# Cross-attention and gated feed-forward on one core: first tile in banks of its own, gate and up steps over four PSUM banks, and activations 32 bytes further on

## The chip, the cores and the metric

The kernel runs on one core of a Trainium2 chip. The metric is the device time of one execution in microseconds, the median of several runs. Before the change it is 1023.58 us, the median of 3 runs (1022.61 to 1025.23).

## The reference

The input is x (32 batches of 128 rows, 256 wide), a context (32 x 128 x 512) and a row mask. Everything is float32.

```python
# cross-attention, 8 heads of 32
t   = layernorm(x)
src = (ctx @ W_src.T + b_src) * mask        # 512 wide: k | v
q   = (t   @ W_tgt.T + b_tgt) * mask
p   = softmax(where(mask_of_key == 0, -inf, q @ k.T / sqrt(32)))
x1  = x + concat(t, p @ v) @ W_out.T + b_out
# feed-forward, hidden width 1024, weights of -1, 0, 1 with a scale s per output
n   = layernorm(x1)
h   = silu(n @ w1.T * s1) * (n @ w2.T * s2)
h   = gelu(h @ h1.T * t1)
h   = gelu(h @ h2.T * t2)
out = x1 + h @ w3.T * s3
```

## The kernel before, in words

**Tiles.** Two batches of 128 rows make a tile of 256 rows (T), so there are 16 tiles. Two streams of work are interleaved: the feed-forward of tile f, the attention of tile a = f + 1, and the projections of tile n = f + 2. Each engine has its own list of instructions, written out by hand; semaphores tie them together. PER (before line 30) says how far a tile moves each semaphore, and at(name, tile, k) is the value to wait for.

**TensorE.** For a tile f, gates_part issues the scores of tile a, then four gate_up steps. A step q computes two blocks of 128 gate columns into bank F[0] and two up blocks into F[1], 8 matmuls each: two blocks, two slices of 128 of the contraction, and a high and a low part. The activations are kept as two float32r tensors (x2h and x2l; hAh and hAl; hBh and hBl) whose sum is the float32 value, while the ternary weights W1, W2, H1, H2, W3 are exact in float32r. Then come transposes_x(n), project_k(n), project_q(n) and project_v(n) in float32. They use the banks G[0] (transposes, q) and G[1] (k, v). middle_part(f) has eight steps of 32 float32r matmuls (q from 4 to 11, banks F[q % 2]), with attend(a) and out_proj(a) ahead of q = 8 and transpose_x2(a) ahead of q = 10, then ffn_out(f). The eighth bank group S takes four banks for the scores.

**Waits of the gate steps.** gate_up(q) waits for sil_ready up to 2q before it writes F[0] again, and for g_ready up to 2q before it writes F[1] again. project_k waits for x1_ready of two tiles before, transposes_x for x2_ready.

**ScalarE.** silu(f, q) (lines 605 to 609), copies of PSUM (copy_xnT, keep_xnT, scale_v, copy_upd, x2_hi), the exponentials exps(a, j) (line 635) and gelu(f, q) (line 616). Each change of function set loads a table (ACT_TABLE_LOAD). silu waits for gate_done first and for g_ready second.

**VectorE.** In the gates' stretch of tile f: keep_residual (line 723), mask_scores(a, 0) (778), gate_times_up (840) for the pairs of blocks, split (857 and 859, the copy that rounds to float32r and the subtraction that gives the low part), then row_max(a, 0) (782, 786), bias_mask_k(n) (754) and the rest of the softmax: normalise (790, 793) and turn_blocks (805), whose result goes through DRAM and back (turn_p on SyncE) to be transposed.

**GpSimd.** The powers -1/2 of both LayerNorms (987, 998), add_bias (994), and in the first tiles the copies cast (1012), which turn each raw float32 weight chunk into float32r in place.

**The start.** The weights come in 22 chunks of 512 KB (4 of W1 and W2, which are EARLY, 8 of H1, 8 of H2, 2 of W3). Before a chunk is cast, an engine looks at the low 16 bits of its elements: look on ScalarE (667) for 19 of them, on VectorE (874) for chunks 9 to 11. count_low_bits, sum_low_bits (1002) and raise_flag (884) make of it two flags, one for the early chunks and one for all. TensorE loads each flag (585, 593) and branches to a float32r or a float32 version of the program. Tile 0 and tile 1 have their own order: first_gates holds the transposes of the probabilities of tile 0 (394), its attention and output projection in G[0] and G[1], projections of tile 1, and then gates_part(0, 1, 2). Tile 1's x and context are loaded into the home of hBh. All transfers are issued on SyncE's queue; its loads start at line 264, s3 is issued last (291).

Of the kernel before, what the change touches and what calls it, by code (L numbers as in the profile page):

```python
# [12 lines left out]
NB = 2  # L13
# [9 lines left out]
WARM = 10  # L23
MASKED = -3.0e38
# [7 lines left out]
    pb_ready=2, p_written=16, p_loaded=64, av_done=1, upd_ready=1,  # L32
    o_done=1, x1_ready=1, stats2=4, veps2=1, rstd2=1, xn2_ready=2, x2t_done=1, x2hi_ready=1, x2_ready=1,
# [5 lines left out]
def program(nc, x, ctxT, mask_row, mask_col, wsT, wvT, wtT, woT, b_cols, b_v, b_out, w1T, w2T, h1T, h2T,  # L39
            w3T, s_cols, s3, out):  # L40
    st = ExitStack()
    with st:
# [49 lines left out]
        hBl = sb("hBl", [P, KH, T], F32R)  # L92
        g, sil = sb("g", [P, 2, 2, T]), sb("sil", [P, 2, T])
# [3 lines left out]
        x_in_1 = tile1_home[:, KC:KC + NB * D // T, :]  # L97

# [3 lines left out]
        def x_of(a):  # L102
            return x_in_1 if isinstance(a, int) and a == 1 else x_in[:]

        F = [st.enter_context(nc.psum_tensor(f"F{i}", [P, 2, T], F32)) for i in range(2)]
# [3 lines left out]
        p_banks = [[F[c][:].rearrange("p h t -> p (h t)") for c in range(KD)],  # L109
                   [S[:, c].rearrange("p j c s -> p (j c s)") for c in range(KD)]]  # L110
# [4 lines left out]
        x_loaded = sem("x_loaded")  # L115
        ctx_loaded = sem("ctx_loaded")
        mrow_loaded = sem("mrow_loaded")
        mcol_loaded = sem("mcol_loaded")
# [83 lines left out]
        on_dve = [9, 10, 11]  # L202
        on_act = [n for n in range(CHUNKS) if n not in on_dve]
# [9 lines left out]
        def _(sp):  # L213
# [4 lines left out]
            def load_mask_row(m):  # L218
                sp.wait_ge(kT_ready, at("kT_ready", m - 1, 2))
                sp.wait_ge(qT_ready, at("qT_ready", m - 1, 2))  # L220
                sp.wait_ge(mask_bias_ready, at("mask_bias_ready", m - 1, 1))
                sp.dma_start(mrow[:], mask_row[bass.ds(m, 1)].broadcast_to([P, T])).then_inc(mrow_loaded, 16)
# [5 lines left out]
            def load_x(m):  # L228
                sp.wait_ge(xn_ready, at("xn_ready", m - 1, 2))
                sp.wait_ge(xb_ready, at("xb_ready", m - 1, 2))  # L230
                sp.dma_start(x_in[:], x[bass.ds(m, 1)].rearrange("o p n -> (o p) n")).then_inc(x_loaded, 16)
# [34 lines left out]
            sp.dma_start(WK[:], wsT).then_inc(wk_loaded, 16)  # L266
            sp.dma_start(bcols[:], b_cols).then_inc(bias_loaded, 16)
            sp.dma_start(mrow[:], mask_row[0:1].broadcast_to([P, T])).then_inc(mrow_loaded, 16)
# [3 lines left out]
            sp.dma_start(mcol[:], mask_col[0]).then_inc(mcol_loaded, 16)  # L272
            sp.dma_start(bv_bc[:], b_v.broadcast_to([P, D])).then_inc(bv_loaded, 16)
            sp.wait_ge(x_loaded, 16)
            sp.dma_start(x_in_1, x[1]).then_inc(x_loaded, 16)
            sp.wait_ge(ctx_loaded, 16)
            sp.dma_start(cT_1.rearrange("p k t -> p (k t)"), ctxT[1]).then_inc(ctx_loaded, 16)
            load_chunks(range(EARLY))
            sp.dma_start(WO[:], woT).then_inc(wo_loaded, 16)
            load_chunks(range(EARLY, EARLY + KH))  # L280
            load_mask_row(1)
            sp.wait_ge(x_loaded, 32)
            sp.wait_ge(xn_ready, at("xn_ready", 0, 2))
            sp.wait_ge(xb_ready, at("xb_ready", 0, 2))
            sp.dma_start(x_in[:], x[2]).then_inc(x_loaded, 16)
            sp.wait_ge(ctx_loaded, 32)
            sp.wait_ge(v_done, at("v_done", 0, 1))
            sp.dma_start(cT[:], ctxT[2]).then_inc(ctx_loaded, 16)
# [795 lines left out]
```

## Time and profile before

| | |
|---|---|
| median of 3 runs | 1023.58 us |
| the profiled execution, its own time | 1028.29 us |
| its span, first to last instruction | 1026.5 us |
| TensorE busy | 962.8 us, 7716 matmuls |
| VectorE, ScalarE, GpSimd busy | 597.4, 393.8, 68.8 us |
| granted TensorE clock, mean | 0.982 |
| moved by DMA | 64.56 MB |

The profile comes from one execution; its time is 4.7 us above the median of the runs shown. A share of the span is an average over the start (about 130 us with gaps) and fifteen tiles that look alike. Where a line of the timeline ends in brackets, they hold the idle time of the engine just before it and what ended it. Matmuls overlap in the pipeline, so the step from one's start to the next's counts, not the duration of one.

### The profile page before, as it was taken

To read this page: it belongs to the slowest core of one execution; us is meant where nothing else is said; L and a number is where in the kernel's file an instruction comes from. 1 tells how busy PE (TensorE), PEld (TensorE's weight loads), DVE (VectorE), ACT (ScalarE), POOL (GpSimd) and SP (SyncE) were. 2 spreads that over 40 slices of the span, in tenths; PEclk is the share of its full clock that TensorE was granted. 3 is DMA by queue.
4 is the path that set the end of the run, shared out by engine and by line. 5 is a ranking of instruction groups with operands and counts; after the bars stand their busy time and mean duration, and the time that the engine had idled before them with its cause. 6 is when DMAs were issued, how large, how long until landed. Compare 5 with 4: busy or idle time off the path is not lost.

```text
span 1026.5 us, 20570 instructions
## 1 busy us (share of the span) xinstructions
PE 962.8 (94%) x7716; PEld 909.0 (89%) x7716; DVE 597.4 (58%) x1143; ACT 393.8 (38%) x1081; POOL 68.8 (7%) x95
## 2 busy tenths in 40 slices
PE   7667899999999999999999999999999999997998
PEld 6567889999898999989899998989999898997888
DVE  4557375575847557484655748466574746657342
ACT  4446243352524335252342525334252533425221
POOL 2133000001000000100001010000101000000000
PEclk9788999999999999999999999999999999999999
DMA  9702103030120303012030301203020130202000
GB/s 335 308 5 83 38 11 109 21 107 10 56 72 10 107 20 107 10 56 72 10 107 20 102 15 46 82 10 107 20 92 26 34 94 10 82 11 76 8 11 11
DMA packets 51438, 64.56 MB, mean 63 GB/s; under 512 B 6736, under 2 KB 43984, under 8 KB 51408
## 3 DMA queue, kind: packets, MB, share of 16 engines
q1 hardware_dynamic: 51408, 64.15, 19.0%
q8 instruction: 20, 0.33, 0.1%
q14 instruction: 10, 0.08, 0.0%
HBM read 44.21 MB, written 19.92 MB: 62 GB/s over the span
## 4 chain that ended last, share of the span: by engine, by line
PE 84%; issue 5%; ACT 4%; DMA 3%; DVE 2%; SPq 1%; ACTq 0%; POOL 0%; DVEq 0%
PE F L456 56%; PE G L438 6%; PE F L525 6%; PE G L370 5%; PE G L348 4%; PE G L359 2%; ACT sil L609 2%; PE S L383 2%; PE G L419 1%; DMA p_dram<-pb 1%; DMA W_raw<-w 1%; ACT pr L635 1%; DVE pr L793 1%; PE G L335 1%; PE G L448 1%
## 5 line engine op out<-in xcount | busy, mean ns | idle before, releaser
L456 PE MATMUL F<-hAh,H 128*128 128x256 f32 x1024 | 251.5, 287 | 11.6 <-POOL H L1012 6.0
L456 PE MATMUL F<-hBh,H 128*128 128x256 f32 x1024 | 250.9, 287 | 0.7 <-DVE hBl L859 0.7
L456 PE MATMUL F<-hAl,H 128*128 128x256 f32 x1024 | 248.1, 284 | 0.0
L616 ACT ACTIVATE g<-F,scols 128x256 f32<-128x256 f32 x256 | 107.2, 471 | 365.8 <-PE F L456 365.6
L456 PE MATMUL F<-hBl,H 128*128 128x256 f32 x1024 | 246.9, 283 | 0.0
L456 PEld LDWEIGHTS F<-hAh,H 128*128 128x128 f32 x1024 | 197.7, 193 | 13.7 <-POOL H L1012 6.4
L456 PEld LDWEIGHTS F<-hAl,H 128*128 128x128 f32 x1024 | 197.8, 193 | 0.3
L456 PEld LDWEIGHTS F<-hBh,H 128*128 128x128 f32 x1024 | 196.1, 192 | 1.3 <-DVE hBl L859 0.9
L456 PEld LDWEIGHTS F<-hBl,H 128*128 128x128 f32 x1024 | 196.3, 192 | 0.4
L456 PE MATMUL F<-x2h,W 128*128 128x256 f32 x512 | 132.8, 298 | 20.5 <-ACT sil L609 18.8
L456 PEld LDWEIGHTS F<-x2h,W 128*128 128x128 f32 x512 | 96.8, 189 | 32.6 <-ACT sil L609 26.1
L456 PE MATMUL F<-x2l,W 128*128 128x256 f32 x512 | 125.5, 282 | 0.0
L635 ACT ACTIVATE pr<-pr,nmx 128x128 f32<-128x128 f32 x256 | 99.1, 388 | 36.8 <-DVE nmx L786 36.8
L857 DVE CAST hAh<-g 128x512 fp32r<-128x512 f32 x128 | 54.0, 422 | 100.6 <-ACT g L616 100.6
L456 PEld LDWEIGHTS F<-x2l,W 128*128 128x128 f32 x512 | 97.1, 190 | 0.0
L857 DVE CAST hBh<-g 128x512 fp32r<-128x512 f32 x64 | 27.2, 426 | 114.1 <-ACT g L616 114.1
L859 DVE TENSOR_TENSOR hAl<-g,hAh 128x512 fp32r<-128x512 f32 x128 | 88.7, 693 | 4.4
L840 DVE SCALAR_TENSOR_TENSOR g<-F,scols,sil 128x256 f32<-128x256 f32 x128 | 56.1, 479 | 58.9 <-PE F L456 39.0
L609 ACT ACTIVATE sil<-F,scols 128x256 f32<-128x256 f32 x128 | 53.7, 470 | 73.4 <-PE F L456 73.2
L525 PE MATMUL F<-W,hAh 128*128 128x256 f32 x256 | 62.1, 283 | 0.0
L525 PE MATMUL F<-W,hAl 128*128 128x256 f32 x256 | 62.1, 283 | 0.0
L998 POOL TENSOR_TENSOR rs<-ve,neg_half 128x2 f32<-128x2 f32 x16 | 11.0, 690 | 692.1 <-DVE ve L820 692.1
(93 smaller groups left out, 1250.2 us busy)
## 6 DMA issues: line engine op xcount, KB each, us to landing
p_dram<-pb SPq DMA_DIRECT2D x30, 512.0 KB, 3.2
pr<-p_dram SPq DMA_DIRECT2D x120, 128.0 KB, 2.6
H_raw<-h SPq DMA_DIRECT2D x16, 512.0 KB, 15.6
cT<-ctx_t SPq DMA_DIRECT2D x15, 512.0 KB, 3.5
out<-y SPq DMA_DIRECT2D x32, 128.0 KB, 1.7
x_in<-x_t SPq DMA_DIRECT2D x15, 256.0 KB, 2.6
W_raw<-w SPq DMA_DIRECT2D x6, 512.0 KB, 10.3
mrow<-mask_row SPq DMA_DIRECT2D x16, 128.0 KB, 3.2
```

The source lines that it names most:

```text
L348: ins = mm(G[1][:, c * T:(c + 1) * T], WK[:, k, c * P:(c + 1) * P], cT_of(a)[:, k, :], start=k == 0, stop=k == KC - 1)
L359: ins = mm(G[0][:, c * T:(c + 1) * T], WQ[:, k, c * P:(c + 1) * P], xnT[:, k, :], start=k == 0, stop=k == KD - 1)
L370: ins = mm(G[1][:, j * D:(j + 1) * D], cT_of(a)[:, k, j * P:(j + 1) * P], WV[:, k, :], start=k == 0, stop=k == KC - 1)
L438: ins = mm(G[1][:, j * D:(j + 1) * D], lhsT, WO[:, k, :], start=k == 0, stop=k == 2 * KD - 1)
L456: return mm(bank, W[0][:, k, cols], part[:, k, :], start=first, stop=last)
L525: ins = mm(F[j][:, 0, :], lhsT, W3[:, k, :], start=first, stop=last)
L609: fn(sil[:, p % 2, :], F[0][:, p % 2, :], ACT.Silu, scale=scols[:, p:p + 1]).then_inc(sil_ready, 1)
L616: fn(g[:, q % 2, m, :], F[q % 2][:, m, :], ACT.Gelu, scale=scols[:, col:col + 1]).then_inc(gelu_ready, 1)
L635: ins = fn(pr[j][:, r, c, :], pr[j][:, r, c, :], ACT.Exp, bias=nmx[:, j, h:h + 1], scale=SCALE, accum_out=den[:, j, h:h + 1])
L840: V.scalar_tensor_tensor(g[:, q % 2, p % 2, :], F[1][:, p % 2, :], scols[:, KH + p:KH + p + 1], sil[:, p % 2, :], ALU.mult, ALU.mult).then ...
L857: V.tensor_copy(hi[:, pair, :], g[:, q % 2, :, :]).then_inc(hi_ready, 1)
L859: V.tensor_tensor(lo[:, pair, :], g[:, q % 2, :, :], hi[:, pair, :].bitcast(F32), ALU.subtract).then_inc(h_ready, 1)
```

## The change

1. **Four banks for gate and up.** Steps q = 0 and 2 write gate and up into G[0] and G[1], steps 1 and 3 into F[0] and F[1]. A step from q = 2 on waits for the SiLU and product of two steps before. sil has four places instead of two. transposes_x(n) and project_k(n) now wait for all sil_ready and g_ready of the tile. silu and gelu have their waits in the other order. VectorE's order is product, split, product, split, product, row_max(a, 0), product, split, split, mask_scores(a, 1).
2. **First tile.** Its attention, output projection and second LayerNorm go batch by batch (j = 0, 1), in banks of their own: tail_banks are two banks of S, o_banks are G[0] and G[1]. Semaphores from av_done to x2_ready count two per tile. Projections q and v and the scores of tile 1 move behind the gates of tile 0, project_k is cut into two halves.
3. **Looks.** ScalarE looks at 14 chunks, VectorE at eight (3, 7, 11, 17 to 21), placed between other work. The casts are in the order of the chunks. The order of the first loads changes; tile 1's mask row gets its own place.
4. **A pad** of 8 float32 (32 bytes) stands before x2h, so x2h, x2l, hA, hB, g, sil and y start 32 bytes further on.

```diff
+PAD = 8
+        sb("pad", [P, PAD])
         x2h, x2l = sb("x2h", [P, KD, T], F32R), sb("x2l", [P, KD, T], F32R)
...
-        g, sil = sb("g", [P, 2, 2, T]), sb("sil", [P, 2, T])
+        hBl, mrow_home = with_raw("hBl", KH, T)
+        g, sil = sb("g", [P, 2, 2, T]), sb("sil", [P, 4, T])
...
+        tail_banks = [s_bank(2), s_bank(3)]
+        o_banks = [G[0], G[1]]
+        def gate_banks(q):
+            if q % 2:
+                return F[0][:], F[1][:]
+            return G[0][:].rearrange("p (h t) -> p h t", h=2), G[1][:].rearrange("p (h t) -> p h t", h=2)
...
-        on_dve = [9, 10, 11]
-        on_act = [n for n in range(CHUNKS) if n not in on_dve]
+        on_act = [0, 1, 2, 4, 5, 6, 8, 9, 10, 12, 13, 14, 15, 16]
+        on_dve = [3, 7, 11, 17, 18, 19, 20, 21]
...
@@ sync: first loads
             sp.dma_start(WV[:], wvT).then_inc(wv_loaded, 16)
+            load_chunks(range(EARLY))
+            sp.dma_start(bv_bc[:], b_v.broadcast_to([P, D])).then_inc(bv_loaded, 16)
+            sp.dma_start(mcol[:], mask_col[0]).then_inc(mcol_loaded, 16)
+            sp.dma_start(x_in_1, x[1]).then_inc(x_loaded_1, 16)
+            sp.dma_start(cT_1.rearrange("p k t -> p (k t)"), ctxT[1]).then_inc(ctx_loaded_1, 16)
             sp.dma_start(bo_bc[:], b_out.broadcast_to([P, D])).then_inc(bo_loaded, 16)
             sp.dma_start(WO[:], woT).then_inc(wo_loaded, 16)
+            sp.dma_start(mrow_1, mask_row[1:2].broadcast_to([P, T])).then_inc(mrow_loaded_1, 16)
+            load_chunks(range(EARLY, EARLY + 4))
+            sp.dma_start(scols[:], s_cols).then_inc(scales_loaded, 16)
+            load_chunks(range(EARLY + 4, EARLY + KH))
             sp.wait_ge(v_done, at("v_done", 0, 1))
+            load_x(2)
             sp.dma_start(cT[:], ctxT[2]).then_inc(ctx_loaded, 16)
+            load_mask_row(2)
             load_chunks(range(EARLY + KH, CHUNKS))
...
@@ tensor: project_k, transposes_x
-                    pe.wait_ge(x2_ready, at("x2_ready", a - 2, 1))
+                    pe.wait_ge(sil_ready, at("sil_ready", a - 2, KH))
...
-                    pe.wait_ge(x1_ready, at("x1_ready", a - 2, 1))
+                    pe.wait_ge(g_ready, at("g_ready", a - 2, KH))
...
@@ tensor: gate_up
-                    pe.wait_ge(sil_ready, at("sil_ready", f, 2 * q))
+                elif q > 1:
+                    pe.wait_ge(sil_ready, at("sil_ready", f, 2 * q - 2))
...
-                    pe.wait_ge(g_ready, at("g_ready", f, 2 * q))
+                elif q > 1:
+                    pe.wait_ge(g_ready, at("g_ready", f, 2 * q - 2))
...
@@ tensor: gates_part of tile 0, first_gates
+                if first:
+                    project_q(1)
+                    scores(1)
+                    project_v(1)
...
                 transpose_p_0(0)
+                out_proj_x_0(0)
+                out_proj_x_0(1)
+                transpose_p_0(1)
+                attend_0(0)
+                attend_0(1)
+                out_proj_u_0(0)
+                out_proj_u_0(1)
                 transposes_x(1)
+                project_k(1, 0)
+                transpose_x2_0(0)
+                transpose_x2_0(1)
+                project_k(1, 1)
                 gates_part(0, 1, 2, general)
...
@@ scalar: silu
+                    act.wait_ge(g_ready, at("g_ready", f, max(p - 3, 0)))
+                    act.wait_ge(gate_done, at("gate_done", f, q + 1))
+                    fn(sil[:, p % 4, :], gate_bank[:, p % 2, :], ACT.Silu, scale=scols[:, p:p + 1]).then_inc(sil_ready, 1)
...
@@ vector: tile
+                if first:
+                    ln1_stats(2)
                 gate_times_up(f, 0)
+                split(f, 0)
                 gate_times_up(f, 1)
+                split(f, 1)
                 gate_times_up(f, 2)
+                if a is not None and not first:
+                    row_max(a, 0)
+                if first:
+                    ln1_apply(2)
+                    look(17)
                 gate_times_up(f, 3)
                 split(f, 2)
+                if first:
+                    look(18)
                 split(f, 3)
+                if first:
+                    look(19)
+                    bias_mask_q(1)
+                    mask_scores(1, 0)
+                    row_max(1, 0)
                 if a is not None:
+                    mask_scores(a, 1)
...
@@ gpsimd: start
             inverse_std1(0)
+            for n in range(EARLY):
+                cast(n)
+            sum_low_bits(0)
             add_bias(0)
             inverse_std1(1)
+            inverse_std2_0(0)
+            inverse_std2_0(1)
+            for n in range(EARLY, EARLY + 4):
+                cast(n)
+            inverse_std1(2)
+            for n in range(EARLY + 4, EARLY + KH):
+                cast(n)
             add_bias(1)
+            for n in range(EARLY + KH, CHUNKS - 2):
+                cast(n)
             sum_low_bits(1)
```

## Rows read from the trace of the kernel before

**Rows 1.** The page: busy time of each engine; GB/s in 40 slices of 25.7 us.

```profile
PE 962.8 (94%) x7716; PEld 909.0 (89%) x7716; DVE 597.4 (58%) x1143; ACT 393.8 (38%) x1081; POOL 68.8 (7%) x95
...
GB/s 335 308 5 83 38 11 109 21 107 10 56 72 10 107 20 107 10 56 72 10 107 20 102 15 46 82 10 107 20 92 26 34 94 10 82 11 76 8 11 11
```

**Rows 2.** Timeline of TensorE, one repeating tile: start us, us, engine, line, operation.

```profile
256.25 0.38 PE L456 MATMUL F<-x2h,W 128*128 128x256 f32 x1
...
257.42 0.28 PE L456 MATMUL F<-x2l,W 128*128 128x256 f32 x1
...
258.14 0.28 PE L456 MATMUL F<-x2l,W 128*128 128x256 f32 x1
...
259.75 0.39 PE L456 MATMUL F<-x2h,W 128*128 128x256 f32 x1 [1.34 <-ACT sil L609]
...
266.30 0.60 PE L335 MATMUL G<-ident,xn 128*128 128x128 f32 x4
266.74 3.62 PE L348 MATMUL G<-cT,WK 128*128 128x256 f32 x16
270.19 1.89 PE L359 MATMUL G<-xnT,WQ 128*128 128x256 f32 x8
...
316.49 0.38 PE L456 MATMUL F<-x2h,W 128*128 128x256 f32 x1
```

**Rows 3.** Timeline of TensorE, the start.

```profile
35.06 1.94 PE L394 MATMUL F<-ident,pr 128*128 128x128 f32 x8 [9.08 <-issue]
...
53.93 0.39 PE L456 MATMUL F<-x2h,W 128*128 128x256 f32 x1 [0.31 <-DVE x2l L832]
...
87.72 0.55 PE L456 MATMUL F<-hAh,H 128*128 128x256 f32 x1 [6.00 <-POOL H L1012]
...
108.93 0.93 PE L419 MATMUL G<-pr,v 128*32 128x128 f32 x16 [3.13 <-DMA pr<-p_dram]
```

**Rows 4.** Timeline of ScalarE in the tile of rows 2.

```profile
257.56 1.28 ACT L609 ACT_TABLE_LOAD   x1 [5.23 <-PE F L456]
...
267.63 1.28 ACT L635 ACT_TABLE_LOAD   x1
271.06 0.40 ACT L635 ACTIVATE pr<-pr,nmx 128x128 f32<-128x128 f32 x1 [2.15 <-DVE nmx L786]
```

**Rows 5.** Timeline of VectorE in the tile of rows 2.

```profile
256.72 1.22 DVE L778 TENSOR_TENSOR pr<-S,mbias 128x1024 f32<-128x1024 f32 x1
...
264.31 0.88 DVE L840 SCALAR_TENSOR_TENSOR g<-F,scols,sil 128x256 f32<-128x256 f32 x2 [0.33 <-PE F L456]
265.11 0.42 DVE L857 CAST hAh<-g 128x512 fp32r<-128x512 f32 x1
...
268.44 0.42 DVE L857 CAST hAh<-g 128x512 fp32r<-128x512 f32 x1
...
269.51 1.21 DVE L782 TENSOR_REDUCE mx<-pr 128x8 f32<-128x1024 f32 x1
...
271.12 0.88 DVE L754 SCALAR_TENSOR_TENSOR kT<-G,bcols,mrow 128x256 f32<-128x256 f32 x2
```

**Rows 6.** SyncE's issue of the last first load, s3, and its time to landing.

```profile
35.18 1.11 SPq L291 DMA_DIRECT2D s_bc<-s  x1
...
DMA to landing us min/median/max: 14.9/14.9/14.9
```

**Rows 7.** Timeline of VectorE, the start: looks, second flag, one normalise.

```profile
40.20 3.46 DVE L874 TENSOR_REDUCE low_bits<-H_raw 128x1 f32<-128x1024 uint16 x3
...
82.96 0.14 DVE L884 TENSOR_SCALAR flag<-most 1x1 int32<-1x1 f32 x1 [0.42 <-POOL most L1002]
...
86.89 6.96 DVE L793 TENSOR_TENSOR pr<-pr,rden 128x1024 f32<-128x1024 f32 x1
```

**Rows 8.** Timeline of GpSimd, the last casts.

```profile
82.89 7.91 POOL L1012 CAST H<-H_raw 128x1024 fp32r<-128x1024 f32 x8
90.75 2.02 POOL L1012 CAST W<-W_raw 128x1024 fp32r<-128x1024 f32 x2
```

More of the change, by code:

```diff
@@ L378, in scores @@
                 pe.wait_ge(masked, at("masked", a - 1, 2))
+                if isinstance(a, int) and a == 1:
+                    pe.wait_ge(x2_ready, at("x2_ready", 0, 2))
                 for j in range(NB):
@@ L529, in gates_part @@
             def gates_part(f, a, n, general):
-                if a is not None:
+                first = isinstance(f, int) and f == 0
+                if a is not None and not first:
                     scores(a)
@@ L582, in _ @@
             project_v(0)
-            project_k(1)
             pe.wait_ge(flag_ready, 1)
@@ L668, in look, with tile @@
                        accum_out=low_bits[:, n:n + 1]).then_inc(act_looked, 1)
-            def tile(f, a, n, looks=()):
+            def tile(f, a, n):
+                first = isinstance(f, int) and f == 0
                 for q in range(4):
                     silu(f, q)
-                if n is not None:
+                    if first:
+                        look(on_act[6 + 2 * q:8 + 2 * q])
+                if not first and n is not None:
                     copy_xnT(n)
-                look(looks)
                 if a is not None:
@@ L884, in raise_flag, with tile @@
                 V.tensor_scalar_min(flag[:, i:i + 1], most[:, i:i + 1], 1.0).then_inc(flag_ready, 1)
-            def tile(f, a, n, m, late_flag=False):
+            def tile(f, a, n, m):
+                first = isinstance(f, int) and f == 0
                 keep_residual(f)
-                if a is not None:
+                if a is not None and not first:
                     mask_scores(a, 0)
+                if first:
+                    ln1_stats(2)
                 gate_times_up(f, 0)
+                split(f, 0)
                 gate_times_up(f, 1)
-                split(f, 0)
+                split(f, 1)
                 gate_times_up(f, 2)
-                split(f, 1)
+                if a is not None and not first:
+                    row_max(a, 0)
+                if first:
+                    ln1_apply(2)
+                    look(17)
                 gate_times_up(f, 3)
                 split(f, 2)
+                if first:
+                    look(18)
                 split(f, 3)
-                if late_flag:
-                    ln1_stats(n)
-                    ln1_apply(n)
-                if a is not None:
-                    row_max(a, 0)
+                if first:
+                    look(19)
+                    bias_mask_q(1)
+                    mask_scores(1, 0)
+                    row_max(1, 0)
+                if a is not None:
+                    mask_scores(a, 1)
+                if first:
+                    row_max(1, 1)
+                    bias_v(1)
+                    for c in on_dve[6:]:
+                        look(c)
                 if n is not None:
                     bias_mask_k(n)
-                if a is not None:
-                    mask_scores(a, 1)
+                if a is not None and not first:
                     row_max(a, 1)
```

382 lines of the change are left out of this document (216 added, 166 removed).

## The prediction

> **What bounds the kernel now.** I read the page first, then the timeline of one repeating tile engine by engine, then the start up to 136 us. TensorE is busy 94% of the span [rows 1], so a term counts only if it takes idle time from TensorE or makes its instructions shorter. Both are to be seen in the tile that starts at 256.25 [rows 2]: from 257.42 to 258.14 six float32r matmuls go by, 0.12 us each; the second gate step waits 1.34 us for the SiLU that still reads its bank; the first matmul of project_k runs at 266.74, 10.49 us after the first gate matmul. The next tile starts at 316.49, so a tile takes 60.24 us. The idle time of the start comes in larger pieces: gaps of 9.1, 6.0 and 3.1 us [rows 3].
>
> **Part 1, four banks for gate and up (tiles 1 to 13).** The 64 matmuls of the gates need 64 x 0.12 = 7.7 us; before they take 10.05 (266.30 - 256.25), so 2.3 us of waits are in reach. In the new order of waits the gate's own wait stands last, on the activation itself. That is how exps is written, and there the table load runs at 267.63, straight behind the copy, while the activation waits until 271.06 [rows 4]. So I let the 1.28 us load of Silu (257.56, after the gate was done) vanish behind idle ScalarE time, and the first SiLU start 1.4 us after the tile instead of 2.6.
> But TensorE then meets a new wait. project_k writes G[1], which is now an up bank, and needs all eight g_ready, given by VectorE. VectorE in the tile's first stretch, in start-to-start steps of [rows 5], from tile start: the residual's copy; mask_scores 0.47 to 1.71 (1.22 and a step); first gate_times_up when the first up step is done, 16 matmuls and 0.28 of drain, 2.25, and 0.80 long: 3.05; split 1.07 (268.44 to 269.51): 4.12; second up product 4.15 to 4.95; split 6.02; third 6.08 to 6.88; the row_max that is put in here, 269.51 to 271.12 = 1.61 (less 0.1): 8.4; fourth 9.2. project_k starts at 9.25 and its first matmul 0.1 later, 9.35 against 10.49: **1.14 us per tile, not 2.3**; the other half comes back as this wait of about 1.3 us, between the transposes (done at 8.4) and project_k. Queued behind it are project_q and project_v, which just shift with it. VectorE runs on without a gap to kT: splits to 11.3, mask_scores to 12.6, while project_k ends at 9.35 + 16 x 0.216 + 0.4 = 13.2. 13 x 1.14 = 14.8 us.
> Tile 14 has no next projection and tile 15 no attention: the middle steps start at the last split. Before, that is 13.3 after tile start (269.51 - 256.25); after, 9.2 + 2.1 = 11.3 for tile 14 and 11.0 for tile 15, whose VectorE is free of mask and maximum. 2.0 + 2.3 = 4.3 us. Sum of this part -19.1 us.
>
> **Part 2, the start.** TensorE stands 9.1 us before 35.06 [rows 3], for the first flag and the branch on it. The change puts this flag earlier: the four early chunks are issued ahead of x[1], cT[1] and two bias loads, 1.0 MB, 3.0 us at the 335 GB/s of the page's first slice [rows 1]; normalise (1.2) goes behind the flag, as does add_bias(0) on POOL, and a look of 1.15 comes before it. I put the flag 3 us earlier. Own banks then shorten transposes, attention, output projection and LayerNorm, and the gates could start near 47 instead of 53.93. This gain is mostly not collected: VectorE waits for s3 before tile 0, s3 is the last transfer, it lands at 35.18 + 14.9 = 50.1 [rows 6], and nothing is taken out of that queue; SyncE's new order (mask row 1 into a place of its own without a wait, x[2] and cT[2] after the first v_done, scols up front) only turns loads around within it. So VectorE starts tile 0 at 50.1; before it started with the gates, at 53.8.
> From there VectorE and TensorE go in turns, with the durations of [rows 2, 5] (a look 3.46 / 3 = 1.15 [rows 7]): four products, four splits, ln1 of tile 2 and looks 17 to 19 end at 63.4; qT(1) 64.3; scores 65.5; masks and maxima 71.1; V(1), at twice 0.216 for half of it since TensorE stood before, 71.1, vb 71.9; K(2) 75.5; exps and the three copies on ScalarE 76.8; Q(2) 78.7; normalise and flag 81.5; V(2) 82.2. The branch on the second flag, written at 83.1 [rows 7], costs what it does now, 87.72 - 83.1 = 4.6: middle steps at 86.7, before 87.72, **-1.0 us**. The wait of attend for its DMA, 3.1 us [rows 3], goes, since that normalise was held until 93.9 and will run at about 84: **-3.1 us**.
> Against it stands a hold on VectorE. normalise at 86.89 takes 6.96 us [rows 7] instead of 1.22, while POOL casts without a pause from 82.89 to 92.77 [rows 8]. In the changed kernel POOL's casts 8 to 14 and add_bias(1) are let go by inverse_std1(2), and this follows ln1_stats(2) on VectorE, right before split(0,0), which subtracts two SBUF tiles. POOL has seven casts of 1.04 and 1.5 us of bias ready then, 8.8 us. Bounds: 0, if POOL leaves pauses, and 8.8. I take what the one row of such a hold shows, 6.96 - 1.22 = 5.7: **+5.7 us**. The head comes to +1.6. The Trainium skill (page "SBUF — State Buffer", section "Who interferes with whom") says that a VectorE instruction with two SBUF inputs and a GpSimd one that reads SBUF can't run together, and that the one which comes second waits for the whole of the other. By that rule, one cast at a time, the hold would be about 1 us and the sum 1001; the 6.96 us, longer than any single cast, don't agree with it.
> Looks themselves: ScalarE gives up five of them, which hides behind the banks' waits; VectorE takes five more, and they are in the list above.
>
> **Part 3, 32 bytes.** Adding up the tensors in order, each rounded up to 32 bytes, x2h, x2l, hA, hB, g, sil and y start on multiples of 64 before and 32 beyond one after; W1 to W3 stay on multiples of 64. So moving and stationary operand stop being alike in position in all 352 float32r matmuls of a tile, 5632 in all. No row has a float32r matmul so placed. The nearest, in float32: project_k, moving cT at 32 and WK at 0, 0.216 us each (3.62 - 0.38 for 15 steps); project_q, both at 0, also 0.216, from 1.89 - 0.38 for 7 [rows 2]. They say nothing happens, and I take **0**. But float32r stands at 0.12 where a float32 transpose of 128 columns, its moving identity at 32 and its stationary xn at 0, steps 0.11 (0.44 for four, 266.30 to 266.74). So the gain is bounded by 0.12 - 0.108 = 12 ns, half of 0.216. A loss isn't excluded; I give it the same 12 ns.
>
> **The sum.** -19.1 + 1.6 = -17.5 us on the profiled execution, 1028.29 (span 1026.5 and 1.8 around it): 1010.8. That execution stands 4.7 above the median 1023.58 of the runs; carried over, 1006.
>
> **Rivals.**
> A, no hold: POOL leaves a gap and VectorE isn't stopped. Against it: normalise's 6.96 us [rows 7]. 1006 - 5.7 = 1000.
> B, the 32 bytes do it: something between the two operand streams costs 12 ns per matmul now. For it: the 0.12 against 0.108. The gates' 64 gain nothing (VectorE sets project_k's start), 288 x 16 x 12 ns = 55 us: 951; a third of it 988. The Trainium skill (page "TensorE: Matmul & The Clock Gate", section "Back-to-back issue gap") gives 262 cycles for 256 moving columns, 109 ns; this case's 120 differs from it, and the measurement decides. By that figure there would be 11 ns to win somewhere.
> C, the steady gain is lost: the load of the Silu table stays behind the gate's wait (0.9 us later for the first product and so for project_k) or VectorE needs 1.1 us more. For it: every step there is tight. 1006 + 14.8 = 1021.
> D, the other side: the shifted operands slow the float32r stream. It decides from 17.5 / 5632 = 3.1 ns on; at 12 ns 1006 + 55 = 1061. Against it: the float32 rows, and no row that is slower by position.
> That the change doesn't do what it says: the pad might move tensors that no bank or port cares about. That is the forecast's own case for part 3.
>
> **The numbers.** Forecast 0.40, A 0.15, B 0.28, C 0.12, D 0.05. About 0.3% (3 us) is what a measurement tells from no change: forecast, A, B and most of C lie beyond, so faster 0.91; same 0.05, from C and the small end of D; slower 0.04. The range goes down to B's full price, 948, and up to 1018, the forecast with 8.8 us of hold and half of C; the forecast's own range is 998 to 1014.
>
> **What would show it.** Project_k's first matmul at 9.3 after tile start with g_ready as its releaser, and the Silu load before the gate is done: part 1. If K comes at 8.5, VectorE isn't the limit. VectorE's first subtraction of tile 0 lasting some us under casts: the hold. First look: the step between float32r matmuls. If it isn't 0.12, the forecast is wrong by 4.6 us for each ns.

## The result, and the profile after

The changed kernel takes 997.86 us, the median of 4 runs (995.59 to 998.0), against 1024.18 for the kernel before beside it on the same chip (4 runs, 1022.61 to 1025.23): a ratio of 0.9734 with a 95% interval of 0.9713 to 0.9755. It is faster, 8 us beyond the forecast of 1006 and inside its range. The profiled execution has a span of 996.0 us against 1026.5.

The page after, the line that answers to the first of [rows 1]: TensorE has lost 29.6 us of busy time with the same 7716 matmuls, nearly the whole 30.5 us by which the span is shorter. So most of the gain isn't idle time that the page shows; either the instructions became shorter or they waited less while they counted as busy.

```profile
PE 933.2 (94%) x7716; PEld 887.0 (89%) x7716; DVE 601.4 (60%) x1151; ACT 388.5 (39%) x1073; POOL 72.3 (7%) x96
```

Timeline of TensorE after, one repeating tile (start us, us, engine, line, operation; answers to [rows 2]):

```profile
250.90 0.38 PE L519 MATMUL G<-x2h,W 128*128 128x256 f32 x1
251.12 0.28 PE L519 MATMUL G<-x2l,W 128*128 128x256 f32 x1
...
251.82 0.28 PE L519 MATMUL G<-x2l,W 128*128 128x256 f32 x1
...
258.69 0.66 PE L372 MATMUL G<-ident,xn 128*128 128x128 f32 x4
260.64 3.69 PE L386 MATMUL G<-cT,WK 128*128 128x256 f32 x16 [1.29 <-DVE g L964]
...
309.36 0.38 PE L519 MATMUL G<-x2h,W 128*128 128x256 f32 x1
```

The tile takes 309.36 - 250.90 = 58.46 us instead of 60.24. The gates need 7.8 us instead of 10.05 (from 250.90 to the transposes at 258.69). The 1.34 us wait for the SiLU is gone, and a wait of 1.29 us for VectorE's last product stands ahead of project_k, which starts 9.74 us after the start of its tile instead of 10.49. From 251.12 to 251.82 six steps take 0.70 us, where [rows 2] show 0.72 for six; experiment 1 reads this over sixty.

The SiLUs and their table load in the same tile after (answers to [rows 4]); and VectorE's part (answers to [rows 5]):

```profile
246.98 1.28 ACT L689 ACT_TABLE_LOAD   x1
252.14 0.84 ACT L689 ACTIVATE sil<-G,scols 128x256 f32<-128x256 f32 x2 [3.88 <-PE G L519]
```

```profile
251.37 1.22 DVE L875 TENSOR_TENSOR pr<-S,mbias 128x1024 f32<-128x1024 f32 x1
253.27 0.88 DVE L964 SCALAR_TENSOR_TENSOR g<-G,scols,sil 128x256 f32<-128x256 f32 x2 [0.69 <-PE G L519]
254.18 0.43 DVE L983 CAST hAh<-g 128x512 fp32r<-128x512 f32 x1
254.65 0.69 DVE L985 TENSOR_TENSOR hAl<-g,hAh 128x512 fp32r<-128x512 f32 x1
255.25 0.87 DVE L964 SCALAR_TENSOR_TENSOR g<-F,scols,sil 128x256 f32<-128x256 f32 x2
...
257.23 0.87 DVE L964 SCALAR_TENSOR_TENSOR g<-G,scols,sil 128x256 f32<-128x256 f32 x2
258.02 1.21 DVE L879 TENSOR_REDUCE mx<-pr 128x8 f32<-128x1024 f32 x1
...
259.61 0.88 DVE L964 SCALAR_TENSOR_TENSOR g<-F,scols,sil 128x256 f32<-128x256 f32 x2
```

The table load runs 4 us before the tile begins, as forecast. VectorE goes in the order forecast, without a gap from 253.27 on.

TensorE in the start after (answers to [rows 3]); no idle time stands before attend at 109.03 any more:

```profile
30.75 1.94 PE L434 MATMUL F<-ident,pr 128*128 128x128 f32 x8 [11.66 <-issue]
...
45.94 0.47 PE L519 MATMUL G<-x2h,W 128*128 128x256 f32 x1
...
69.06 2.09 PE L424 MATMUL S<-kT,qT 32*128 32x128 f32 x32 [9.07 <-issue]
...
91.36 0.55 PE L519 MATMUL F<-hAh,H 128*128 128x256 f32 x1 [3.64 <-issue]
...
109.03 1.08 PE L486 MATMUL G<-pr,v 128*32 128x128 f32 x32
```

VectorE and GpSimd in the start after (answer to [rows 7, 8]; s3, issued at 34.30, lands 15.0 us later, which is 49.3, [rows 6]):

```profile
49.41 0.43 DVE L820 COPY res<-x 128x512 f32<-128x512 f32 x1 [2.21 <-issue]
...
51.96 1.20 DVE L983 CAST hAh<-g 128x512 fp32r<-128x512 f32 x1
53.19 1.41 DVE L985 TENSOR_TENSOR hAl<-g,hAh 128x512 fp32r<-128x512 f32 x1
...
58.01 1.76 DVE L837 TENSOR_SCALAR xn<-x_in,mv,rs 128x256 f32<-128x256 f32 x2
...
68.10 0.86 DVE L860 SCALAR_TENSOR_TENSOR qT<-G,bcols,hBl_raw 128x256 f32<-128x256 f32 x2
...
86.55 0.13 DVE L1010 TENSOR_SCALAR flag<-most 1x1 int32<-1x1 f32 x1
```

```profile
51.84 4.92 POOL L1160 CAST H<-H_raw 128x1024 fp32r<-128x1024 f32 x4
56.72 1.84 POOL L1139 TENSOR_TENSOR xb<-hBh_raw,bo_bc 128x256 f32<-128x256 f32 x2
58.52 7.99 POOL L1160 CAST H<-H_raw 128x1024 fp32r<-128x1024 f32 x7
```

While GpSimd casts, the split's cast takes 1.20 us instead of 0.43, its subtraction 1.41 instead of 0.69 (the same lines at 254.18 and 254.65), the LayerNorm's two passes 1.76 instead of 0.73.

**Where the 30.5 us of span went**, by the start of each tile in the two traces: tile 1's gates begin 1.55 us earlier (133.96 instead of 135.51), tiles 1 to 13 take 23.3 us less in all (tile 1 2.02, each of the others 1.76 to 1.78), and from tile 14's gates to the end it is 5.6 less. The next section separates the causes inside these.

### The profile page after: what moved, and what is told of

It is laid out like the page before. It is cut to its first block, busy times and chain, and to the rows that moved or that the text cites. A ratio compares the mean times of both kernels' runs of the same rounds, so it can differ in the third digit from the quotient of the medians.

```text
span 996.0 us, 20724 instructions
## 1 busy us (share of the span) xinstructions
PE 933.2 (94%) x7716; PEld 887.0 (89%) x7716; DVE 601.4 (60%) x1151; ACT 388.5 (39%) x1073; POOL 72.3 (7%) x96
## 4 chain that ended last, share of the span: by engine, by line
PE 83%; DVE 7%; issue 5%; DMA 1%; ACT 1%; SPq 1%; POOL 0%; DVEq 0%; ACTq 0%
PE F L519 49%; PE F L593 6%; PE G L503 6%; PE G L386 5%; PE G L519 5%; PE G L409 5%; PE G L398 3%; DVE g L964 3%; DVE mx L879 2%; PE S L424 2%; PE G L486 1%; PE G L511 1%; DMA p_dram<-pb 1%; ACT pr L716 1%; DMA WK<-wk 1%
## 5 line engine op out<-in xcount | busy, mean ns | idle before, releaser
L519 PE MATMUL F<-hBh,H 128*128 128x256 f32 x1024 | 244.8, 283 | 0.8 <-DVE hBl L985 0.8
L519 PE MATMUL F<-hAl,H 128*128 128x256 f32 x1024 | 243.7, 281 | 0.0
L519 PE MATMUL F<-hBl,H 128*128 128x256 f32 x1024 | 240.6, 279 | 0.0
L519 PEld LDWEIGHTS F<-hBh,H 128*128 128x128 f32 x1024 | 191.8, 187 | 1.4 <-DVE hBl L985 1.0
L386 PE MATMUL G<-cT,WK 128*128 128x256 f32 x240 | 55.6, 384 | 19.1 <-DVE g L964 16.3
L386 PEld LDWEIGHTS G<-cT,WK 128*128 128x128 f32 x240 | 44.3, 190 | 27.6 <-issue 20.3
L519 PE MATMUL G<-x2h,W 128*128 128x256 f32 x256 | 63.6, 287 | 0.7 <-DVE g L964 0.7
L519 PE MATMUL F<-x2h,W 128*128 128x256 f32 x256 | 61.8, 280 | 1.3 <-DVE g L964 1.3
L519 PE MATMUL G<-x2l,W 128*128 128x256 f32 x256 | 61.8, 279 | 0.0
L519 PE MATMUL F<-x2l,W 128*128 128x256 f32 x256 | 61.7, 280 | 0.0
```

What stands on the lines that cost most here:

```text
L386: ins = mm(G[1][:, c * T:(c + 1) * T], WK[:, k, c * P:(c + 1) * P], cT_of(a)[:, k, :], start=k == 0, stop=k == KC - 1)
L519: return mm(bank, W[0][:, k, cols], part[:, k, :], start=first, stop=last)
```

## The experiments

Times are medians, each with its ratio to the runs of the kernel before beside it. "K" is the start of project_k after the start of its tile, "the period" the time from one tile's gates to the next; both are medians over the repeating tiles of the trace.

**1. The pad alone, taken out and put in.** First the changed kernel without it:

```diff
-        sb("pad", [P, PAD])
         x2h, x2l = sb("x2h", [P, KD, T], F32R), sb("x2l", [P, KD, T], F32R)
```

> The changed kernel without the pad, so that the activations start on multiples of 64 bytes again. Theory 1 (the 32 bytes shorten the float32r step): the step goes back from about 117 to 120 ns, the repeating tile from 58.47 to about 59.33 us (288 matmuls x 3.0 ns), K's start after the gates stays near 9.75, and the time rises by 13 to 14 us, to about 1011. Rival (the shorter step came from something else in the change, the bank order or the waits): step 117, tile 58.47, time 998.

Measured: 1011.0 us (1007.56 to 1011.69), ratio 0.9861 [0.9834, 0.9889]; period 59.35, K at 9.76, span 1008.9. Then the kernel before with a pad of 32 bytes and nothing else:

```diff
+        sb("pad", [P, 8])
         x2h, x2l = sb("x2h", [P, KD, T], F32R), sb("x2l", [P, KD, T], F32R)
```

> The kernel before with nothing but the pad ahead of x2h. Theory 1: step 117 instead of 120 ns also here, tile 60.24 to about 59.2, time 1024 to about 1008 to 1011. Rival (the pad needs the rest of the change): tile 60.24, time 1024.

Measured: 1011.72 us (1010.69 to 1012.74), ratio 0.988 [0.9859, 0.99]; period 59.41, K at 10.45. The middle steps of one tile in four kernels, each time the first and the sixty-first matmul of an unbroken row (timeline of TensorE). First the kernel before:

```profile
336.04 0.28 PE L456 MATMUL F<-hAl,H 128*128 128x256 f32 x1
...
343.22 0.28 PE L456 MATMUL F<-hAl,H 128*128 128x256 f32 x1
```

The changed kernel without the pad:

```profile
330.98 0.28 PE L518 MATMUL F<-hAl,H 128*128 128x256 f32 x1
...
338.17 0.28 PE L518 MATMUL F<-hAl,H 128*128 128x256 f32 x1
```

The changed kernel:

```profile
330.73 0.28 PE L519 MATMUL F<-hAl,H 128*128 128x256 f32 x1
...
337.73 0.28 PE L519 MATMUL F<-hAl,H 128*128 128x256 f32 x1
```

The kernel before with the pad alone:

```profile
330.73 0.28 PE L457 MATMUL F<-hAh,H 128*128 128x256 f32 x1
...
337.73 0.28 PE L457 MATMUL F<-hAh,H 128*128 128x256 f32 x1
```

Sixty steps take 7.18 and 7.19 us without the pad (120 ns each) and 7.00 with it (117 ns), in either kernel. So the pad by itself is worth 13.1 us in the changed kernel (1011.0 - 997.9) and 12.5 in the kernel before (1024.2 - 1011.7), and the rest of the change another 13.2 (1024.2 - 1011.0) by the medians.

**2. What of the position counts.** The pad put ahead of all tensors, so that weights and activations both move by 32 bytes and their distance stays as it was before:

```diff
+        sb("pad", [P, PAD])
         W1, W1_raw = with_raw("W1", KD, HID)
...
-        sb("pad", [P, PAD])
         x2h, x2l = sb("x2h", [P, KD, T], F32R), sb("x2l", [P, KD, T], F32R)
```

> The changed kernel with the pad ahead of W1 instead of ahead of x2h, so that weights and activations both start 32 bytes beyond a multiple of 64. Theory 1a (what counts is the distance of the moving from the stationary operand): alike in position again, step 120 ns, tile 59.35, time 1011. Rival 1b (what counts is where the moving operand lies by itself): step 117, tile 58.47, time 998.

Measured: 1009.12 us (1008.82 to 1010.4), ratio 0.9845 [0.9821, 0.9869]; period 59.35, step 120 ns. Where the activations lie by themselves does nothing; what counts is how far they lie from something ahead of them in memory. In a float32r matmul that is the weights. The pad moves the activations away from every other tensor ahead of them too, so another engine that reads those tensors at the same time is a rival. The traces speak against it: of the middle steps from 300 to 900 us, those during which VectorE, ScalarE and GpSimd all stand idle take 120.0 ns on the average without the pad (665 steps) and 117.0 with it (650 steps). Next, 64 bytes in the place of 32:

```diff
-PAD = 8
+PAD = 16
```

> The pad is 64 bytes instead of 32, at the same place. Theory 1a, that 32 bytes between the position of the weights and that of the activations matter as such (in units of 64 bytes): 64 bytes put them back as they were, so the step is 120 ns, the period 59.35 us and the time 1011, as without a pad. Rival, that any shift against the weights helps: the step is 117 ns, the period 58.5 and the time 998.

Measured: 998.98 us (998.39 to 1000.39), ratio 0.975 [0.9718, 0.9781]; periods of 58.32 and 58.61 in turn, steps of 117 and 118 ns. My theory that it goes by units of 64 bytes fell. Adding up the sizes of all tensors in order, the activations began at an exact multiple of 512 bytes from the weights in the kernel before (162304 bytes for x2h, and 0, 8192, 16384, 49152 and 81920 for W1, W2, H1, H2 and W3). Last, 256 bytes, in the fastest of the kernels below:

```diff
-PAD = 8
+PAD = 64
```

> The kernel with all of the earlier moves (six silu and products, casts held, kT first, s3 waited for late: 970.0, period 56.75 us, float32r step about 117 ns), with a pad of 256 bytes instead of 32. Without a pad the activations lie at a multiple of 512 bytes from the weights; with 32 and with 64 bytes more the step falls from 120 to 117 ns. Theory of a short pattern, where the distance counts modulo 128 or 256 bytes: 256 bytes are as bad as none, so the step is 120 ns and the time about 970 + 12 = 982. Theory of a long one, where it counts modulo 512 or more: the step is 117 ns or less and the time 970; were the whole excess over a float32 transpose's 109 ns to go, 110 ns, 288 x 7 ns = 2.0 us less per tile and about 938.

Measured: 985.6 us (985.1 to 986.01), ratio 0.9623 [0.9607, 0.9639], that is 15.6 us more than the same kernel with 32 bytes (969.97, experiment 8); period 57.71 instead of 56.75, which makes 12.5 us in tiles 1 to 13. Timeline of TensorE, the first and the fortieth matmul of an unbroken row:

```profile
340.31 0.28 PE L519 MATMUL F<-hBl,H 128*128 128x256 f32 x1
...
344.98 0.28 PE L519 MATMUL F<-hBh,H 128*128 128x256 f32 x1
```

39 steps in 4.67 us are 120 ns again. So 0 and 256 bytes beyond a multiple of 512 give 120 ns, 32 and 64 give 117. A pattern that repeats every 128 or every 256 bytes would fit these four points; no other distance was tried, and what in the chip makes the difference stays open.

**3. Are four banks needed?** The changed kernel with gate and up back in F[0] and F[1] and the waits that belong to them; everything else stays, the order of waits on ScalarE and of work on VectorE too:

```diff
-            if q % 2:
-                return F[0][:], F[1][:]
-            return G[0][:].rearrange("p (h t) -> p h t", h=2), G[1][:].rearrange("p (h t) -> p h t", h=2)
+            return F[0][:], F[1][:]
...
-                    pe.wait_ge(sil_ready, at("sil_ready", a - 2, KH))
+                    pe.wait_ge(x2_ready, at("x2_ready", a - 2, 2))
...
-                    pe.wait_ge(g_ready, at("g_ready", a - 2, KH))
+                    pe.wait_ge(x1_ready, at("x1_ready", a - 2, 2))
...
-                    pe.wait_ge(sil_ready, at("sil_ready", f, 2 * q - 2))
+                    pe.wait_ge(sil_ready, at("sil_ready", f, 2 * q))
...
-                    pe.wait_ge(g_ready, at("g_ready", f, 2 * q - 2))
+                    pe.wait_ge(g_ready, at("g_ready", f, 2 * q))
```

> The changed kernel with all gate and up steps back in F[0] and F[1], with the waits of before on these banks, and transposes and project_k free of the wait for sil_ready and g_ready; the order of the waits in silu (table load early) and everything else stay. Theory 2 (the steady gain is that of four banks, less the wait of project_k): without them the gates take about 9.3 to 10 us, project_k starts at 10 to 10.5, tile 59 to 59.2, time 1006 to 1010. Rival (the early table load alone does it; four banks only trade a wait on SiLU for a wait on the products): gates 8.4 to 8.8, project_k at 8.9 to 9.3 instead of 9.74, tile 57.6 to 58.0, time 986 to 992.

Measured: 993.35 us (990.1 to 993.73), ratio 0.9688 [0.9662, 0.9714]; period 57.98, gates 8.89, K at 9.32. Four banks, with the waits that the change gives them, cost 4.5 us. ScalarE in this kernel (timeline):

```profile
244.79 1.28 ACT L687 ACT_TABLE_LOAD   x1
249.96 0.84 ACT L687 ACTIVATE sil<-F,scols 128x256 f32<-128x256 f32 x2 [3.88 <-PE F L517]
```

The load begins 5.2 us before the SiLU, so it runs early here too. The period is 2.26 us below that of the kernel before, of which the pad makes 0.9 by experiment 1; the other 1.4 come without four banks.

**4. The order of silu's two waits alone**, put back to that of the kernel before, in the changed kernel:

```diff
-                    act.wait_ge(g_ready, at("g_ready", f, max(p - 3, 0)))
                     act.wait_ge(gate_done, at("gate_done", f, q + 1))
+                    act.wait_ge(g_ready, at("g_ready", f, max(p - 3, 0)))
```

> The changed kernel with silu waiting for gate_done first and g_ready second, as before. Theory 5 (the wait written last rides on the activation, and the table load runs ahead of it): the Silu table load falls behind the gate again, the first product comes about 0.9 us later, project_k at 10.6 instead of 9.74, tile 59.3, time 1010. Rival (four banks cover the load): project_k at 9.7 to 9.8, tile 58.5, time 998.

Measured: 1019.17 us (1017.64 to 1022.54), ratio 0.9951 [0.9925, 0.9977]; K at 10.48, as expected, but the period is 60.88 where 59.3 was expected. Timelines of ScalarE and TensorE, and busy times and granted clock by window (the columns are in its head line):

```profile
193.25 1.28 ACT L689 ACT_TABLE_LOAD   x1 [5.25 <-PE G L519]
```

```profile
261.62 5.38 PE L386 MATMUL G<-cT,WK 128*128 128x256 f32 x16 [1.95 <-DVE g L964]
266.83 1.89 PE L398 MATMUL G<-xnT,WQ 128*128 128x256 f32 x8
```

```profile
core 0: us, PE busy (x) PEld busy (x) DVE busy (x) ACT busy (x) POOL busy (x), PEclk, DMA share, GB/s
261.60:266.80 5.20, 5.18 (x16) 4.27 (x17) 3.06 (x5) 3.33 (x17) 0.00 (x0) 0.67 0.00 0
266.80:268.50 1.70, 1.70 (x9) 1.49 (x9) 1.30 (x3) 0.00 (x0) 0.00 (x0) 1.00 0.00 0
```

The load again comes after the first gate, and only then the SiLU. The wait before project_k has grown from 1.29 to 1.95 us, and the granted clock over the 5.2 us behind it is 0.67 instead of 1.00: part of them ran at 1.2 GHz, the lower of the two levels. Project_k takes 5.38 us in this tile where the changed kernel has 3.69, so 1.69 more, close to the 1.6 by which the period exceeds what was expected. Not all tiles show it. In eight of tiles 1 to 13 project_k takes 5.38 us and the period is 60.7 to 61.0; in the other five, with waits of the same length (1.95 to 1.96 us), it takes 3.69 us and the period is 59.2 to 59.3, as expected. What decides between them stays open. By the traces tiles 1 to 13 take 23.5 us more than in the changed kernel: about 10 by the late SiLU itself (13 x 0.74, the difference of K) and 13.5 by the clock (8 x 1.69). By the medians the place of one line on ScalarE is worth 21 us of this kernel.

**5. VectorE's maximum behind the fourth product:**

```diff
-                if a is not None and not first:
-                    row_max(a, 0)
...
                 gate_times_up(f, 3)
+                if a is not None and not first:
+                    row_max(a, 0)
```

> The changed kernel with row_max(a, 0) back behind the fourth gate_times_up in the repeating tiles. Theory 3 (project_k waits 1.3 us for VectorE's fourth product, which stands behind this maximum): project_k at 8.9 to 9.1 instead of 9.74, tile about 57.8, time about 989. Rival (the exponentials, now 0.9 us later, hold up something behind): no gain or under 3 us, with a new wait in attend or the splits.

Measured: 990.57 us (988.52 to 993.18), ratio 0.9663 [0.964, 0.9686]; K at 8.95, period 57.99. The wait before project_k falls to about 0.5 us: VectorE is what K waits for.

**6. Six instead of eight.** The last gate step writes F[0] and F[1]; G[0] and G[1] were last used by the third, so six SiLUs and six products are enough for the transposes and project_k:

```diff
-                    pe.wait_ge(sil_ready, at("sil_ready", a - 2, KH))
+                    pe.wait_ge(sil_ready, at("sil_ready", a - 2, KH - 2))
...
-                    pe.wait_ge(g_ready, at("g_ready", a - 2, KH))
+                    pe.wait_ge(g_ready, at("g_ready", a - 2, KH - 2))
```

> The changed kernel with transposes_x(n) and project_k(n) waiting for six instead of eight sil_ready and g_ready: G[0] and G[1] are last used by step q = 2, steps 1 and 3 are in F. Theory 3 (project_k waits for the fourth product, which its bank doesn't need): project_k's first matmul at 8.2 to 8.3 after the gates' start instead of 9.74, tile 57.0 to 57.3 (project_v may wait 0.3 us for kT), time 977 to 982. Rival (VectorE's work up to kT is the limit, whatever lets project_k go): project_v waits over 1 us for kT, tile 57.8 to 58.5, time 990 or more.

Measured: 980.9 us (979.96 to 983.22), ratio 0.957 [0.9543, 0.9597]; K at 8.08, period 57.33. Timeline of TensorE:

```profile
255.16 0.60 PE L372 MATMUL G<-ident,xn 128*128 128x128 f32 x4
255.59 3.62 PE L386 MATMUL G<-cT,WK 128*128 128x256 f32 x16
259.05 1.89 PE L398 MATMUL G<-xnT,WQ 128*128 128x256 f32 x8
261.29 0.89 PE L409 MATMUL G<-WV,cT 128*128 128x256 f32 x3 [0.35 <-DVE kT L851]
```

No wait is left before K; a small one stands before V, for kT. This is what four banks are good for: 17.0 us faster than the change as it was made, and 12.5 faster than experiment 3 with the two old banks.

**7. GpSimd's casts held back in tile 0** until its fourth split is written:

```diff
             inverse_std1(2)
+            pool.wait_ge(h_ready, 4)
             for n in range(EARLY + 4, EARLY + KH):
```

> The changed kernel with one more wait: GpSimd begins with cast 8 and what follows only when the four splits of tile 0 are done. Theory 4 (casts hold VectorE's copies and subtractions of tile 0, 1.2 and 1.41 us instead of 0.43 and 0.69): VectorE's chain from the first to the last split becomes 4 to 5 us shorter, the second flag and the middle steps come 3 to 5 us earlier than 91.4, time 993 to 995. Rival (the start is bound by TensorE and by ScalarE's exponentials, or the casts now come late): middle steps at 90 to 92 or later, time 997 to 1000.

Measured: 993.45 us (991.02 to 995.16), ratio 0.9682 [0.9655, 0.9709]. Timeline of VectorE:

```profile
54.16 0.43 DVE L983 CAST hAh<-g 128x512 fp32r<-128x512 f32 x1
54.62 0.69 DVE L985 TENSOR_TENSOR hAl<-g,hAh 128x512 fp32r<-128x512 f32 x1
...
66.71 0.87 DVE L860 SCALAR_TENSOR_TENSOR qT<-G,bcols,hBl_raw 128x256 f32<-128x256 f32 x2
```

Every split has its own length again, and from the first split to qT it takes 12.55 us instead of 16.14. That is 3.6 less, not the 4 to 5 expected, since three of the products now wait for SiLUs, 1.5 us together. The middle steps start at 90.6, only 0.7 earlier. But in this profiled execution TensorE came out of the first branch at 34.5 us, not at 30.75; tile 1's gates start at 132.20 all the same, against 133.96. The period is the same 58.46. By the medians the change is worth 4.4 us, by the spans 2.6 (996.0 and 993.4), with this later branch in it.

**8. Together.** Experiments 6 and 7, and kT's pass moved ahead of the second masking in the repeating tile:

```diff
+                if n is not None and not first:
+                    bias_mask_k(n)
                 if a is not None:
                     mask_scores(a, 1)
```

> The changed kernel with transposes and K waiting for six silu and six products (worth 17.0 us by itself), POOL's casts from the eighth on held until tile 0's fourth split (worth 4.4 by itself), and kT's pass moved ahead of the second masking in the repeating tile, so that V does not wait for it. If the first two simply add: 997.9 - 17.0 - 4.4 = 976.5. If V's waits of 0.4 to 0.7 us behind kT also go: 13 x 0.5 less, 970. Rival: the second masking, now about 1.5 us later in each tile, delays the exponentials behind it and the gain of the move is lost or worse: 976 to 980.

Measured: 970.92 us (969.53 to 971.91), ratio 0.9474 [0.9442, 0.9505]; period 56.74, tile 1's gates at 128.04. V waits no more (timeline of TensorE):

```profile
249.60 3.62 PE L386 MATMUL G<-cT,WK 128*128 128x256 f32 x16
253.06 1.89 PE L398 MATMUL G<-xnT,WQ 128*128 128x256 f32 x8
254.78 1.46 PE L409 MATMUL G<-WV,cT 128*128 128x256 f32 x6
```

Against experiment 6 tiles 1 to 13 take 7.5 us less and the start 4.7 less, while from tile 14's gates to the end it is 0.7 more; the spans differ by 11.5 (979.7 and 968.2), the medians by 10.0. Last, VectorE's wait for s3 moved to where s3 is used:

```diff
             dve.wait_ge(scales_loaded, 16)
-            dve.wait_ge(s3_loaded, 16)
             tile(0, 1, 2, 3)
...
+                if first:
+                    dve.wait_ge(s3_loaded, 16)
                 scale_out(f, 0)
```

> As the kernel before this one in the list, and VectorE waits for s3 ahead of its first use (scaling the output of tile 0) and not ahead of the whole of tile 0. In the changed kernel VectorE waited until 49.41 us there, 2.2 us of it idle. If that wait is on the path to tile 1: 1.5 to 2.5 us less than the kernel before it. Rival: tile 0's first product waits for TensorE's gate and up steps, which begin at 45.9 and end near 50, so nothing changes: within 1 us.

Measured: 969.97 us (968.28 to 972.69), ratio 0.9472 [0.9439, 0.9505]. The ranges of the two overlap, so the gain is within 1 us and can't be told from none; tile 1's gates start at 127.28 instead of 128.04. VectorE then waits for ScalarE's SiLUs in tile 0 instead. The two versions are 27 and 28 us faster than the changed kernel, and 53 and 54 faster than the one before.

## Why the prediction was right, and where its steps were not

**The total.** The forecast was 1006, measured are 997.86. Its sum over parts 1 and 2, -17.5 on the profiled execution, is what experiment 1 shows without the pad: a span of 1008.9 against 1026.5, -17.6. By the medians the same step is only 13.2, since the profiled execution of the kernel before lay 4.7 above its median; carrying the whole -17.5 over to the median made this part too good by 4. What was missed is part 3. So the 8 us by which the forecast is off are the pad's 13 less the 4 to 5 of this carrying over: two errors that partly cancel.

**Part 3, the step that failed: the pad at 0.** "They say nothing happens, and I take 0", of the float32 rows. The runs show 3 ns per float32r matmul, 120 to 117, and 12.5 to 13.1 us. The float32 rows were no evidence: project_k and project_q step at 216 ns at their two different distances, in every kernel here, and the difference shows in the float32r stream alone. The bound of 12 ns, from the transposes at 0.11, was a bound, and only a quarter of it was there. Of the rivals, B had the sign right; even its third of 4 ns was larger than what came. Of the 3 ns, the share that lies in the gates gains little where VectorE sets K: 288 x 3 ns = 0.86 us per tile, and the period falls by 59.35 - 58.47 = 0.88. The Trainium skill (page "TensorE: Matmul & The Clock Gate", section "Back-to-back issue gap") gives 262 cycles, or 109 ns, for 256 columns as the gap of a single matmul, and says that in a stream with weight loads both set the spacing. No position here reached the 109: the 117 to 118 at 32 and 64 bytes are the lowest medians here.

**Part 1, 1.14 per tile and a new wait before project_k.** The mechanism was right: table load ahead of the tile, no wait in the gates, a wait of 1.3 us for g (measured 1.29) ahead of project_k. K was forecast at 9.35 and came at 9.74. Without the pad the period fell by 60.24 - 59.35 = 0.89 instead of 1.14, and tiles 1 to 13 together by 11.9 us instead of 14.8. The mis-sized term is the step from a product to the split behind it: 0.80 was taken from [rows 5], where the split works on the product of one step earlier; where it needs the product just written it is 254.18 - 253.27 = 0.91. That is 0.1 each for the first two splits, and the first product came 0.12 later than forecast (253.27 - 250.90 = 2.37, not 2.25). The last pieces went nearly as said: tiles 14 and 15 were forecast at -4.3, and without the pad, from tile 14's gates to the end, it is 4.6 less. What I didn't see is that the gain isn't due to the banks. I named the table load as a part of it, but with silu's waits put back K is at 10.48 again, the 10.49 of before (experiment 4), and without the four banks it is at 9.32 (experiment 3); the four banks moved the wait from the gates to K, and did so at a loss, because of a wait for eight where six do (experiment 6).

**Part 2, the start, +1.6.** Measured -1.55 (and -1.2 without the pad). The first flag came 2.7 us earlier (23.33 instead of 25.99), forecast 3, and tile 0's gates start at 45.94, forecast 47. The wait for s3 came as forecast, at 49.41 for 50.1; that it would swallow the gain of the earlier flag is half true, since moving it changes at most 1 us (experiment 8). The hold of VectorE by GpSimd was put at one row's 5.7 us. Its size came out right, in part by luck, since its form was wrong: not one long stop, but one delay per instruction, none over 0.8. The eight instructions that are longer in the changed kernel (two casts by 0.77 and 0.68, four subtractions by 0.7 each, the two LayerNorm passes together by 1.03) sum to 5.4. Experiments 6 and 8 leave the branch alike (30.17 and 30.19) and differ in the held casts: from the first split to qT it is 16.15 us and 10.77, again 5.4, and the scores of tile 1 start at 68.95 and 63.64. The Trainium skill (page "SBUF — State Buffer", section "Who interferes with whom") says the one that comes second waits for the whole of the other instruction. The rows of the changed kernel agree: a GpSimd cast by itself takes 1.03 to 1.04 us, and no delay is longer; and a normalise that starts at 85.41, ahead of a cast at 85.61, keeps its 1.22 us while the cast takes 1.92. I had used it to price a single such delay, 1 us, and would have been wrong by the number of instructions. It doesn't explain the 6.96 us of [rows 7], which the second run of experiment 1 repeats (normalise at 83.68, 6.82 us). In both traces this instruction ends 1.08 us after the last of ten casts in a row, about its own length, so it seems to have waited for all the casts still to come. Why it did so, while the subtractions waited only 0.7 us each, stays open.
The middle steps start at 91.36, forecast at 92.4 (86.7 and 5.7), 1.0 earlier. The branch on the second flag takes 91.36 - 86.55 = 4.8, forecast 4.6. From the middle steps to tile 1's gates it is 42.6 instead of 47.8, 5.2 less, where I counted 3.1 for the wait before attend. A term that I had put at nothing is the clock behind that wait. From attend to the next middle step it is 4.4 us instead of 9.4, 1.9 less beyond the wait of 3.1. In the kernel before, the granted clock is 0.54 over the 2.8 us behind the wait and 0.67 over the next 1.3, which makes about 1.7 us; in the changed kernel it is 1.00 over the same work. This 1.9 and the 1.0 ahead of it make up most of the 3.1 between the forecast of +1.6 and the measured -1.55.

**The errors that cancelled.** Without the pad, part 1 came 2.9 us short in the steady tiles and part 2 was 2.8 better than forecast. That their sum, -17.6, agrees with -17.5 is luck.

**Rivals.** A, no hold, is excluded by the rows and by experiment 7. B, the 32 bytes, came true in its sign and not in its size; the lower end of the range, 948, was said to be B's full price, which by its own sum is 951. C, the steady gain lost, is what experiment 4 builds: 1019 against the 1021 worked out for it, though that rival left out both the pad's gain and the loss of clock. D, a slower float32r stream, didn't come; no kernel had a median step over 120 ns.

## What to carry to other kernels

Measure the step of the commonest matmul and try its operands 32 bytes further apart before reworking a schedule: here it took one line and gave half of the whole gain of 26. Where two sets of functions share ScalarE, let the last wait before the activation be the one that ends last, so that the table load runs ahead of it. And when buffers are rotated, count again who used each last: here a wait for the whole tile, where a part is enough, turned 12.5 us that two more banks can give into a loss of 4.5.

## What the runs showed of the hardware that I had not expected

- A float32r matmul of 256 columns steps at 120 ns where its moving operand lies 0 or 256 bytes beyond a multiple of 512 from its weights, and at 117 to 118 where it lies 32 or 64 bytes beyond; moving both alike changes nothing. The float32 matmuls of the same shape in project_k and project_q, whose distances differ, both step at 216 ns.
- In these kernels a table load waits only for the waits ahead of the last one of its activation: at 246.98, 5.2 us before the SiLU, in one order of the two waits, and after the gate in the other.
- In the kernel of experiment 4 a wait of 1.95 us before project_k was followed by a granted clock of 0.67 over the next 5.2 us, and project_k took 1.69 us longer; this happened in eight of thirteen tiles, whose waits were all 1.8 to 2.0 us long. In the changed kernel, with waits of 1.29 us, it happened in none. It cost more (13.5 us) than the delay itself (about 10).
- Beside GpSimd's casts eight VectorE instructions of the changed kernel were 0.3 to 0.8 us longer each; in the kernel before, one of 1.22 us took 6.96 and ended 1.08 us after the last of the casts.
- TensorE came out of the first branch between 30.2 and 34.5 us, in versions of the changed kernel whose instructions up to there are the same. Such shifts of up to 4 us in one profiled execution are why the terms of the start were read from differences inside a trace.
